# Routed-expert biases: from a one-hot product on TensorE to a broadcast row added by VectorE, with gelu and gate product one round later

## What is computed

```python
def _experts_all(x, g, gb, w1, b1, w2, b2):
    y = jax.nn.gelu(jnp.einsum('bsd,edf->bsef', x, g) + gb, approximate=False)
    y = y * (jnp.einsum('bsd,edf->bsef', x, w1) + b1)
    return jnp.einsum('bsef,efd->bsed', y, w2) + b2
aff = jax.nn.sigmoid(jnp.einsum('bsd,de->bse', x, wa))
topk_p, topk_i = jax.lax.top_k(aff, K)          # K = 2 of E = 16
combine = ...                                    # the two gates, normalised, one column per expert
routed = jnp.einsum('bsed,bse->bsd', _experts_all(x, rg, rgb, rw1, rb1, rw2, rb2), combine)
...
return x + shared + routed                       # then layernorm and residual
```

## Time and profile before

| | us |
|---|---|
| median of 3 runs | 1582.25 |
| lowest, highest | 1580.59, 1585.57 |
| the profiled execution, its own time | 1585.65 |
| its span in the profile | 1583.9 |
| TensorE busy (modelled) | 1442.1 (91%) |
| VectorE busy | 1061.7 (67%) |
| ScalarE busy | 983.1 (62%) |
| GpSimd busy | 549.0 (35%) |

### The profile page before, as it was taken

The page is one execution under the profiler, slowest core; times in us unless marked ns, Lnnn a source line. Parts: engine busy times, 40 slices in busy tenths (PEclk is TensorE's granted clock), DMA queues, the critical chain, the costliest instruction groups (busy, mean ns, idle before and its releaser), DMA issues. The chain is left out here.

```text
span 1583.9 us, 24989 instructions
## 1 busy us (share of the span) xinstructions
PE 1442.1 (91%) x7066; PEld 1001.6 (63%) x7067; DVE 1061.7 (67%) x2119; ACT 983.1 (62%) x2423; POOL 549.0 (35%) x782
## 2 busy tenths in 40 slices
PE   5599999999999999997698979999999999999996
PEld 4364656656575665654476768777777677676774
DVE  4576777777877777774546665387777777773466
ACT  3588787777878777777433011277777777774333
POOL 2112233323323332321212124135656556562024
PEclk9688999989899898987799989999999999999998
DMA  5444566656555664644535333458776766654755
GB/s 167 61 91 66 119 150 106 157 102 128 115 123 146 108 155 82 131 105 121 191 129 186 108 118 108 164 143 237 176 205 143 179 141 136 144 95 78 299 214 207
DMA packets 103696, 222.94 MB, mean 141 GB/s; under 512 B 14228, under 2 KB 40342, under 8 KB 99672
## 3 DMA queue, kind: packets, MB, share of 16 engines
q1 hardware_dynamic: 85864, 179.92, 42.5%
q0 software_dynamic: 17696, 41.43, 13.9%
HBM read 219.20 MB, written 72.35 MB: 184 GB/s over the span
## 5 line engine op out<-in xcount | busy, mean ns | idle before, releaser
L1354 ACT ACTIVATE bank<-bank,mr 128x384 f32<-128x384 f32 (+3 forms) x512 | 254.9, 502 | 28.9 <-DVE mr L1602 28.4
L1602 DVE TENSOR_REDUCE mr<-bank 128x1 f32<-128x512 f32 (+3 forms) x352 | 214.3, 636 | 82.3 <-PE bank L2236 81.5
L1371 ACT ACTIVATE P<-bank 128x512 f32<-128x512 f32 x320 | 181.3, 596 | 82.1 <-PE bank L2250 80.6
L2165 PE MATMUL bank<-cut,xg 128*128 128x512 f32 x632 | 204.5, 405 | 2.6 <-DVE cut L1984 2.6
L1984 DVE TENSOR_TENSOR cut<-ring,cut 128x512 fp32r<-128x512 f32 x316 | 197.4, 687 | 8.3 <-ACT cut L1483 3.9
L2234 PE MATMUL bank<-Ks,Qs 96*128 96x384 f32 (+3 forms) x512 | 164.6, 390 | 37.2 <-ACT P L1371 17.2
L2165 PE MATMUL bank<-xt,ws 128*128 128x512 f32 x768 | 184.0, 398 | 0.8 <-DVE hb L1734 0.8
L1483 ACT ACTIVATE cut<-ring 128x512 fp32r x316 | 173.7, 620 | 5.0 <-issue 3.7
L2048 POOL TENSOR_SCALAR_AFFINE_SELECT P<-P 128x256 f32<-128x256 f32 (+1 forms) x192 | 94.4, 496 | 217.5 <-ACT P L1371 214.1
L2165 PEld LDWEIGHTS bank<-xt,ws 128*128 128x128 f32 x768 | 146.6, 192 | 33.3 <-issue 1.4
L2148 POOL DMA_INDIRECT z_scratch<-wst,pl x79 | 128.4, 1625 | 105.9 <-ACT wst L1504 86.3
(11 more groups left out here) (252 smaller groups left out, 2637.5 us busy)
## 6 DMA issues: line engine op xcount, KB each, us to landing
ring<-in_w SPq DMA_DIRECT2D x79, 1024.0 KB
ring<-in_w SPq DMA_DIRECT2D x79, 512.0 KB
Qs<-st SPq DMA_DIRECT2D x192, 128.0 KB, 5.0
xt<-xt_scratch SPq DMA_DIRECT2D x32, 512.0 KB, 6.4
xt_scratch<-xt SPq DMA_DIRECT2D x30, 512.0 KB, 3.0
xin<-in_x SPq DMA_DIRECT2D x8, 1024.0 KB, 6.8
rd<-rt_scratch SPq DMA_DIRECT2D x64, 128.0 KB, 3.7
xf<-x_scratch SPq DMA_DIRECT2D x8, 1024.0 KB, 9.4
```

The lines of the kernel that those rows point to most:

```text
L1354: m = e.activation(ps[:, o * k:o * k + k], ps[:, o * k:o * k + k], ACT.Exp, scale=-1.0, bias=mr[:, G % 2, c:c + 1], accum_out=se[:, G % 2, ...
L1371: e.activation(Pt[:, p, :], bank[PA.bank[step]][:, :], ACT.Exp, scale=-1.0).then_inc(s_exp, 1)
L1602: e.tensor_reduce(mr[:, G % 2, 0:16].rearrange("p (h i) -> p h i", i=4)[:, h:h + n, i:i + 1], bank[PA.bank["max", b, p, j]][:, 0:n * k].re ...
L2165: m = e.matmul(ps, lhs(a_, k), rhs(b_, k), start=first and k == 0 and j == 0, stop=last and k == n - 1 and j == 2)
```

## The change

The bias product, its one-hot operand and the tile `rb_s` go. A new tile `bb` has a row of 512 biases for each of the five places in the weight ring, repeated over all 128 partitions. SP fills it with a third DMA per fetch that reads one row of `rb` and writes it to 128 partitions. For the first two tiles this is a separate function `fetch_bias`, called ahead of the store of the last shared tile.

VectorE adds `bb` to the whole bank (128x512) and writes the sum to `ub`, in its part of `rup(j)`, once the 12 products are done. Gelu (ScalarE, in place in `ub`) and the gate product (VectorE, in place) become a step of their own, `gate(j-1)`, which stands in plan round j between the second and the third cut. `rturn(j-1)` follows at the end of the same round as before.

```diff
@@ plan_moe
         if j + 1 < NS:
             s = P.add("take", j + 1)
             TR.done(P.on(TR, s))
-            for k in range(4):
+            for k in range(2):
+                P.add("cut", 4 * (j + 1) + k)
+        if 0 <= j - 1 < NS:
+            P.add("gate", j - 1)
+        if j + 1 < NS:
+            for k in range(2, 4):
                 P.add("cut", 4 * (j + 1) + k)
         if 0 <= j < NS:
             s = P.add("rup", j)
@@ SP, fetch_w(j)
+                    if j > 1:
+                        e.dma_start(bb[:, bass.ds(sl, 1), :], rb[bass.ds(ex, 1), :].rearrange("(o e) d -> o e d", o=1).to_broadcast([128, 1, 512]), cond=fl).then_inc(d_wr[j % AHEAD], 16)
+
+            def fetch_bias(j):
+                ex = e.value_load(tab[0:1, 0, j:j + 1], min_val=0, max_val=E - 1)
+                sl = e.value_load(tab[0:1, 1, j:j + 1], min_val=0, max_val=NSLOT - 1)
+                fl = e.value_load(tab[0:1, 2, j:j + 1], min_val=0, max_val=1)
+                e.dma_start(bb[:, bass.ds(sl, 1), :], rb[bass.ds(ex, 1), :].rearrange("(o e) d -> o e d", o=1).to_broadcast([128, 1, 512]), cond=fl).then_inc(d_wr[j % AHEAD], 16)
...
                 elif kind == "down" and n < N1:
+                    if n == N1 - 1:
+                        w.wait_ge(cT_pe, N1)
+                        for j in range(2):
+                            fetch_bias(j)
                     w.wait_ge(zs_dve, n + 1)
@@ ScalarE
-                elif kind == "rup":
+                elif kind == "gate":
                     q = n % 2
-                    w.wait_ge(rup_pe, n + 1)
-                    w.wait_ge(h_dve, N1)
-                    if n >= 2:
-                        w.wait_ge(rh_dve, n - 1)
-                    e.activation(rgl[:, q, :], bank[PM.bank[step]][:, 0:256], ACT.Gelu).then_inc(rgl_act, 1)
+                    w.wait_ge(ub_dve, n + 1)
+                    e.activation(ub[:, q, 0:256], ub[:, q, 0:256], ACT.Gelu).then_inc(rgl_act, 1)
@@ VectorE
                 elif kind == "take":
                     q = n % 2
-                    w.wait_ge(route_dve, 5)
                     if n >= 2:
-                        w.wait_ge(rup_pe, n - 1)
-                    e.tensor_copy(ohj[0:16, q, :], ohs[0:16, n:n + 1].to_broadcast([16, 128])).then_inc(ohj_dve, 1)
-                    e.tensor_copy(ohj[32:48, q, :], ohs[32:48, n:n + 1].to_broadcast([16, 128])).then_inc(ohj_dve, 1)
+                        w.wait_ge(cut_pe, 4 * (n - 1))
...
                 elif kind == "rup":
                     q = n % 2
-                    w.wait_ge(rgl_act, n + 1)
+                    w.wait_ge(cut_pe, 4 * (n + 1))
...
-                    e.tensor_tensor(rhb[:, q, :], bank[PM.bank[step]][:, 256:512], rgl[:, q, :], ALU.mult).then_inc(rh_dve, 1)
+                    e.tensor_tensor(ub[:, q, :], bank[PM.bank[step]][:, :], bb[:, bass.ds(held[n], 1), :].rearrange("p o d -> p (o d)"), ALU.add).then_inc(ub_dve, 1)
+                elif kind == "gate":
+                    q = n % 2
+                    w.wait_ge(rgl_act, n + 1)
+                    e.tensor_tensor(ub[:, q, 256:512], ub[:, q, 256:512], ub[:, q, 0:256], ALU.mult).then_inc(rh_dve, 1)
@@ TensorE
-                                 lambda b_, _: cut[c % NCUT][:, b_, :], first=k == 0, last=False).then_inc(cut_pe, 1)
-                    w.wait_ge(ohj_dve, 2 * n + 2)
-                    w.wait_ge(b_dve, 2)
-                    e.matmul(ps[:, :], ohj[:, q, :], rb_s[:, :], start=False, stop=True).then_inc(rup_pe, 1)
+                                 lambda b_, _: cut[c % NCUT][:, b_, :], first=k == 0, last=k == 3).then_inc(cut_pe, 1)
...
-                        m = e.transpose(ps[:, k * 128:(k + 1) * 128], rhb[:, q, k * 128:(k + 1) * 128], ident[:, :])
+                        m = e.transpose(ps[:, k * 128:(k + 1) * 128], ub[:, q, 256 + k * 128:384 + k * 128], ident[:, :])
```

More of the change, by code:

```diff
@@ L821, in program @@
             assert low + 5 * 12288 + 10240 <= mid
+            bb_at = here()
+            sb2("bb_head", [128, 448])
             comb = sb2("comb", [128, NT, E])
             comb3 = sb2("comb3", [128, NT, 80], F32R)
+            bb = over("bb", [128, NSLOT, 512], bb_at)
+            assert NSLOT * 2048 <= 1792 + 2048 + 320 * N1
             b2_s = sb2("b2_s", [80, 512], F32R)
-            rb_s = sb2("rb_s", [128, 512], F32R)
             xg_at = here()
@@ L933, in bank_free @@
                 w.wait_ge(sem_, PA.nth[(reader, *(was[1:3] if was[0] == "wo" else was[1:]))])
-        moe_read_by = {"up": h_dve, "cT": cT_act, "down": zs_dve, "take": xg_dve, "rup": rh_dve,
+        moe_read_by = {"up": h_dve, "cT": cT_act, "down": zs_dve, "take": xg_dve, "rup": ub_dve,
                        "rturn": hr_act, "rdown": yo_act}
@@ L1215, in fetch_w @@
                 if j < NS:
-                    w.wait_ge(route_dve, 11)
+                    w.wait_ge(route_dve, 9)
                     if j >= NSLOT:
@@ L1438, in _ @@
             attention_over(w)
-            w.wait_ge(d_b, 48)
-            w.wait_ge(pad_dve, 5)
+            w.wait_ge(d_b, 32)
             e.activation(b2_s[:, :], wst[0:80, 1536:2048], ACT.Copy).then_inc(b_act, 1)
-            e.activation(rb_s[0:48, :], wst[0:48, 2048:2560], ACT.Copy).then_inc(b_act, 1)
             w.wait_ge(comb_dve, 2)
@@ L1764, in _ @@
             e.tensor_tensor(b2_s[32:64, :], wst[32:64, 1536:2048], b2_s[32:64, :], ALU.subtract).then_inc(b_dve, 1)
-            w.wait_ge(b_act, 2)
-            e.tensor_tensor(rb_s[32:48, :], wst[32:48, 2048:2560], rb_s[32:48, :], ALU.subtract).then_inc(b_dve, 1)
             w.wait_ge(comb_dve, 1)
@@ L1769, in _ @@
                 e.memset(comb3[:, :, c:c + SH].bitcast(F32), 1.0).then_inc(comb_lo, 1)
-            w.wait_ge(b_act, 3)
+            w.wait_ge(b_act, 2)
             e.tensor_tensor(comb3[:, :, 64:64 + E], comb[:, :, :], comb3[:, :, 0:E], ALU.subtract).then_inc(comb_lo, 1)
-            e.memset(ohs[:, :], 0.0).then_inc(dve_own, chain.up())
-            e.memset(ohj[:, :, :].bitcast(F32), 0.0).then_inc(dve_own, chain.up())
             te, ta, tc, be = sm[:, 0:16], sm[:, 16:32], sm[:, 32:48], sm[:, 48:64]
@@ L1898, in stats @@
                     e.bn_aggr(mv3[:, t, :], bst3[:, PM.ends.stat[t] % 8, :]).then_inc(f_mean, 1)
+            held = {}
             for step in PM.steps:
@@ L1983, in _ @@
                     w.wait_ge(cut_act, n + 1)
-                    e.tensor_tensor(cut[n % NCUT][:, 1:2, :], ring[:, bass.ds(place, 1), 512 * k:512 * k + 512], cut[n % NCUT][:, 0:1, :],
+                    e.tensor_tensor(cut[n % NCUT][:, 1:2, :], ring[:, bass.ds(held[n // 4], 1), 512 * k:512 * k + 512], cut[n % NCUT][:, 0:1, :],
                                     ALU.subtract).then_inc(cut_dve, 1)
@@ L2349, in _ @@
                 elif kind == "cT":
-                    w.wait_ge(b_act, 4)
+                    w.wait_ge(b_act, 3)
                     w.wait_ge(comb_lo, 3)
```

53 lines of the change are left out of this document (19 added, 34 removed).

## The result

| | before | changed |
|---|---|---|
| median of the runs, us | 1582.49 (4 runs, 1580.59 to 1585.57) | 1627.84 (4 runs, 1623.11 to 1629.98) |
| ratio | 1 | 1.028 (95% interval 1.0263 to 1.0297) |
| span of the profiled execution, us | 1583.9 | 1621.4 |

The changed kernel is slower by 45 us; 1626 was forecast, with 1606 to 1645 as the range. Its profiled execution (1623.11) is the shortest of its four, so its span understates the loss.

A forecast was written before the change was run, and what follows sets the result against it. TensorE was taken to bound the routed stage, with rounds of 5.35 us. Terms 38.8 + 0.6 (rounds 1 and 2) + 3 + 1.0 = +43.4 us on the profiled span, 1627.3, adjusted to a median of 1626, range 1606 to 1645.

The forecast's parts named there:

- The bias product goes: Routed rounds: TensorE's own work falls by 0.23 us a round, to 5.12; 18 us if nothing else binds.
- VectorE's add: Routed rounds: the 128x512 bias add, 0.69 us, is hidden by VectorE's idle time; cost 0.
- The gate product behind `xgl` and two cuts: Routed rounds: TensorE waits 0.75 us for the product, so rounds take 5.87 us instead of 5.35; +38.8 us.
- its upper bound: Full rounds: the transposes' weight load could not run ahead behind a wait, at most 0.11 us; +0.63 a round.
- Late cuts: Routed rounds: ScalarE's late first cuts, in 8 rounds, no longer hidden by TensorE's buffers; +3 us (0 to 6).
- The start: Start of routed stage: two bias fetches delay the last store 1.4 us, 0.4 hidden by the cut's wait; +1.0 us.
- The third DMA per fetch: Routed stage: SP's fetch grows to some 3.2 us, under the round's 5.87; 0 (0 to 3).
- round 78: Last full round: no tile to take and no cuts, so it gains 0.23 us.
- The removed routing work: Routing work removed beside a TensorE-bound stage saves nothing; 0 (-1 to 0).
- the full rounds: Rounds j = 3 to 78: 75 x 0.52 - 0.23 = +38.8 us (31.3 to 47.0).
- the real gain: Rival: product in time, TensorE's rounds 5.12 us, total 1565, if `xgl` to first transpose is 1.78 us; chance 0.07.
- The clock: Rival: TensorE falls to half clock in the rounds' waits; one round in ten so gives 1655; chance 0.04.

The follow-up runs named there:

- the order alone: The kernel before, bias product kept on TensorE, with only gelu and gate product moved into the next round behind two cuts; 1627.3 us, rounds of 5.84 us.
- no cut ahead: The changed kernel with the gate step right behind `xgl`, ahead of all four cuts instead of behind two; 1570.7 us, rounds of 5.15 us.
- three cuts ahead: The changed kernel with the gate step behind three cuts instead of two; 1672.2 us, rounds of 6.44 us.
- the best kernel: The changed kernel with the gate step right behind `xgl` and the first two bias fetches behind the last store to z_scratch; 1566.1 us.
- one cut ahead: The changed kernel with the gate step behind one cut instead of two; 1583.2 us, rounds of 5.24 us.
- early-load kernel: The changed kernel with ScalarE's and VectorE's load of the tile's place moved ahead of their waits for the take and `xg`; 1621.2 us.

## Why the prediction was right, and where its terms were off

1. *The bias product goes* (0.23 us a round). It goes, and was worth 0.20: in the kernels that TensorE bounds, rounds are 5.15, not 5.12. In the changed kernel itself it was worth nothing, as the order alone gives the same 5.84.
2. *VectorE's add* (hidden). Right: with no cut ahead the same add stands in a round that VectorE does not lengthen.
3. *The gate product behind `xgl` and two cuts* (5.87 us a round). Right in mechanism and size: 5.84. Of its terms, the way to `xgl` was 3.40 instead of 3.34: the two transposes take 0.44 us behind the wait and took 0.38 without one, a loss that the sum had only in its upper bound. From VectorE's end to the transposes it was 0.06 instead of 0.14. The latter was taken from other transposes, those of `take` at the start of the stage, and does not carry over; why they take longer is open. The length of the wait is not the reason: with three cuts ahead TensorE waits 1.08 us and starts 0.05 us behind VectorE's end (1208.97 to 1209.02). The two errors partly cancel.
4. *Late cuts* (+3). 4.7 us, in 16 rounds rather than 8. The register load that is sometimes long makes 2.6 us of it in five rounds, which is what the forecast mainly priced, without naming it. The rest are eleven rounds, ten of them late by 0.16 to 0.18 us; in nine of the eleven a delay opens between VectorE's first and second cut, which no interval before the change shows, and its cause is not known. The size was in range in part by luck.
5. *The start* (+1.0). Measured +2.9. This term was sized too low in two ways. The two fetches did push the store back, but by about 2.2 us (its data was ready at 1017.50, the store issued at 1019.73) instead of 1.4: from store to store SP took 5.3 us, where the forecast had 4.4 for the fetches. From the store to `xgl` it was then 3.1 us rather than the 2.4 before. And the 0.4 that the first cut was to hide was not there.
6. *The third DMA per fetch* (0). Nothing in the rounds points to it: with the order corrected, rounds with all the bias transfers are TensorE's own.
7. *Not in the sum: the end.* The new step of the last tile stands behind the first shared unit in ScalarE's queue. In the profile this is +2.8 us from the last `xgl` to the last `wst`; its part in the total is open. The forecast counted round 78 as a gain and did not look at what follows it.
8. *The removed routing work* (0). Some 3 us outside the routed rounds, by the comparison under the result; not isolated.

The forecast of 1626 lies 1.8 us under the measured 1627.8, which is closer than its terms deserve. Between the last shared `wst` and the last `wst` it was 4.9 us short (43.4 against 48.3: the full rounds 2.0 too much, late rounds 1.7, the start 2.4 with its four intervals, and the end 2.8 too little), and some 3 us that it did not count on came off elsewhere.

The rivals: the real gain (1565) is what the kernel gives once the gate step stands behind `xgl` (1570.7) and the start is mended (1566.1), so its condition, 1.78 us from `xgl` to the transposes, was what failed. Its sum came out near for mixed reasons: the routed stretch of the best kernel is 10.6 us shorter than before (424.8 against 435.4), not 17, and the rest lies outside it. Measured on either side: with one cut ahead TensorE is just late (5.24 against 5.15), with none it is in time. The clock did not fall in the waits of the rounds: it was 1.00 even with three cuts ahead, where TensorE was idle 1.1 us in each (297.31 of 360 us busy). The rule of the Trainium skill (TensorE: Matmul & The Clock Gate, "A second HAM failure mode: psum-queue depth-cycling"), by which frequent short waits make the clock swing, did not show in this window, which is of the kernel with three cuts ahead:

```profile
1060.00:1420.00 360.00, 297.31 (x1225) 194.66 (x1224) 228.60 (x387) 220.47 (x445) 185.61 (x165) 1.00 0.64 154
```

## What to carry to other kernels

When a step is moved between pipeline rounds, don't ask whether its engine has time, but what now stands ahead of it in that engine's queue and when that can start. If what stands ahead depends on the waiting engine's previous round, the wait feeds back into itself, and the round becomes the length of that ring, whatever work was saved. Here one position in a list, two cuts, turned a gain of 12 us into a loss of 45; the slack of each possible place can be read from one round of the timeline before anything is run. A DMA put ahead of another in an issuing queue costs its register loads too (two small fetches held a store back by 2.2 us), and the last round of a loop has other neighbours than the rest.

## What the runs showed of the hardware beyond the forecast

- The transposes of `rturn` started 0.05 to 0.06 us after VectorE's end, behind waits of 0.52 us (1210.61 to 1210.67), 1.08 us (1208.97 to 1209.02) and 3.29 us (1496.55 to 1496.61). Those of `take` at the start of the stage took 0.14 behind a wait of 0.87 us.
- A register load from `tab`, 0.28 to 0.30 us at the median, took up to 0.94 us in single rounds, on VectorE and on ScalarE, before and after the change. What makes it long is open.
- The same idle time of TensorE, 3.29 us at the end of the routed rounds, went with the half clock in seven profiles and with the full clock in three. Idle times of 2.4 us and more at the start of the stage went with the half clock in all of them.
- Late rounds come in a pattern. In the changed kernel nine of the sixteen start at 1059.0, 1106.7, 1154.4, 1202.2, 1249.3, 1296.8, 1343.7, 1390.6 and 1437.5 us, every eighth round, most of them 0.16 us over; the early-load kernel has nine of its own, every eighth round too, each some 0.28 over. In both the delay opens between VectorE's first and second cut. Its cause was not tested. Before the change none of the 74 intervals is more than 0.12 us over the median: TensorE did not wait for VectorE there.
- Removing a matmul behind a group of 12 saved 0.20 us, though it had 0.23 us in the chain: the 12 took 2.78 us instead of 2.75.
